# Audio tower on one core: small matmuls padded to 128, a hint at the loop's back branch, and new orders for the five engines

## The chip, the cores and the metric

The kernel runs on 1 core of one Trainium2 chip. The metric is device time in microseconds (us) for one execution, and the median of several executions is compared. Everything is float32.

## The reference, cut to what matters

32 clips of 625 frames with 128 samples each go through one DCT and four residual blocks:

```python
h = dct_frames(x)                                   # 625 -> 626 tokens of 128
h = h + bidirectional_mamba2(layernorm(h))          # conv with 4 taps, scan, gate, project
h = h + moe_top2_of_8_experts(layernorm(h))         # hidden 512, exact gelu
h = h + window_attention_8(layernorm(h))            # 8 heads of 16, 8 positions
h = h + pattern_ffn(layernorm(h))                   # gelu, top-64 of 512, gelu, top-128 of 256,
                                                    # softmax, values (256x64), 64 -> 512, top-64
```

In the last block `agg = softmax(top_p) @ process_values` has 64 columns and feeds `gelu(agg @ output_input_weights.T)`. In the Mamba block the depthwise convolution has 256 channels for x and 16 each for B and C, per direction. Every expert adds a bias b2 after its second matmul.

## The kernel before

Each clip is padded to 640 tokens, five tiles of 128. The work of a clip is cut into **four stages**: stage 1 is the DCT and the Mamba block, stage 2 the mixture of experts, stage 3 the window attention, stage 4 the pattern block. The stages are pipelined over clips: the trip of the loop for clip b runs stage 1 of clip b, stage 2 of clip b-1, stage 3 of clip b-2 and stage 4 of clip b-3. Three trips ahead of the loop and three behind it are written out; the loop `Fori(3, 32)` has 29 trips and so 28 taken back branches on each engine.

Every engine has a generator for each stage; a `yield` cuts it into **segments**. Below, "4.19" on an engine is segment 19 of its stage 4, counted from 0. `merged` takes segments in the order of a string of digits, one string for each engine, written out by hand or by a program outside the kernel: digit 4 means "the next segment of stage 4". An engine runs strictly in this order, and a segment that waits for a semaphore holds back all that stands behind it. So the strings alone set who waits for whom.

The segments that the text speaks of, with their lines:

- VectorE (DVE). Stage 1: 1.0 moments of h (L1031 to L1037); 1.1 to 1.4 the arithmetic of dt; from 1.5 on a scan of decays (L1072) and a weighing (L1080, L1083) for each of 12 chunks; 1.29 and 1.30 the Mamba output (L1094, L1102) and its moments. Stage 2: 2.0 moments; 2.1 to 2.3 gate, choice and slots; 2.4 adds the experts' answers (L1158, L1161), the last segment of a trip. Stage 3: 3.0 moments; 3.1 the logits (L1174 to L1180); 3.2 to 3.4 the softmax and values; 3.5 and 3.6 the residual (L1195, L1199) and moments. Stage 4: 4.1 to 4.8 the first top-64 of three tiles, in rounds of three MAX8 (L1219) and three MATCH_REPLACE8 (L1222), and 4.10 to 4.17 of two; 4.19 to 4.27 and 4.29 to 4.37 the split into pairs (L1241 on, L1249, L1252); 4.28 and 4.38 the weighing of it; 4.39 to 4.59 the last top-64; between them the outputs (L1281).
- TensorE (PE). 1.0 transposes x (L527), 1.1 the DCT, 1.5 to 1.43 twenty half units of convolution and gate (L566), 1.44 the wait for the last of them, then for each chunk B and C (L577), transposes (L584), the skip (L594) and the heads (L600); 1.93 to 1.95 project the output (L620, L628). 2.3 and 2.4 turn the routed rows (L663), then `up` (L675) and `down` (L684 with the bias, L686, L663) for 17 expert tiles. 4.1 to 4.5 the patterns (L747); 4.6 to 4.15 transposes (L754) and second matmuls (L762); 4.16 to 4.30 a chain of three for each tile (L772, L777, L782); then L791 and L796.
- ScalarE (ACT) evicts PSUM with the functions of each stage; Silu, Gelu and Exp live in different tables. Its segment 2.2 (L884, L888) reads 17 expert numbers into registers and starts three loads of weights.
- GpSimd (POOL) normalizes (`normalized`, L383 to L388), runs the attention's trees (L460 to L489), gates the Mamba output (L411), scatters and gathers the routed rows by indirect DMA (L442, L450). 1.5 and 1.6 scale the attention output of stage 1 (L425, L428), 1.7 adds it to h (L432, semaphore h1_done), 3.9 is stage 3's second normalization, 3.10 copies h3 into hk (L497).
- SyncE (SP) starts the remaining DMAs, among them the decays through DRAM and the routed rows (L339).

Of the kernel before, what the change touches and what calls it, by code (L numbers as in the profile page):

```python
# [13 lines left out]
P = 128  # L14
# [18 lines left out]
BC = 48  # L33
CW = 2 * P + BC
# [30 lines left out]
    ("ipT", NI), ("pwT", 4 * NP_), ("pv", 2 * HD), ("owT", NO), ("op", 4 * P),  # L65
# [7 lines left out]
for _name, _n in SETUP:  # L73
# [64 lines left out]
def audio_tower(nc, NB, consts_d, setup_d, x_d, out_d, rows_d, experts_d, routed_d, answers_d):  # L138
    ctx = ExitStack()
    with ctx:  # L140
# [64 lines left out]
        Bw = [sb(f"Bw{d}", [NS, CH, P]) for d in range(2)]  # L205
        Cs = [sb(f"Cs{d}", [NS, CH, WIN]) for d in range(2)]
# [46 lines left out]
        aggT = sb("aggT", [HD, P])  # L253
# [40 lines left out]
        def b2_of(i):  # L294
            return expert[i % WR][0:1, 8 * P + KB:EC]
# [58 lines left out]
        def run(engine, order, *stages):  # L354
# [4 lines left out]
            with engine.Fori(last, NB) as b:  # L359
# [140 lines left out]
        def _(pool):  # L500
# [10 lines left out]
            for d in range(2):  # L511
                nc.gpsimd.memset(Bw[d][:, :, WIN:P], 0.0)
# [9 lines left out]
        def pe_stage1(pe, b):  # L522
# [27 lines left out]
            for n in range(HALF_UNITS):  # L550
# [80 lines left out]
        def pe_stage2(pe, b):  # L631
# [47 lines left out]
            def down(i):  # L679
# [4 lines left out]
                nc.tensor.matmul(at, c("ones", 1), b2_of(i), start=True, stop=False)  # L684
# [53 lines left out]
        def pe_stage4(pe, b):  # L738
# [25 lines left out]
            for t in range(TILES):  # L764
# [11 lines left out]
                for j in range(2):  # L776
                    last = nc.tensor.matmul(pD[0:HD, 512:512 + P], c("pv")[:, j * HD:(j + 1) * HD], selT[:, j * P:(j + 1) * P],  # L777
# [4 lines left out]
                nc.tensor.matmul(pD[:, 0:NO], aggT[:], c("owT", HD), start=True, stop=True).then_inc(G["a3_ps"].s, 1)  # L782
# [659 lines left out]
```

## Time and profile before

| | us |
|---|---|
| median of 3 runs | 8329.64 |
| lowest and highest | 8313.04, 8416.84 |
| span of the profiled execution | 8631.7 |
| VectorE busy in it | 6951.3 |
| TensorE busy in it | 6340.7 |
| ScalarE, GpSimd busy in it | 3240.6, 3053.8 |

The profiled execution is one of its own, and its span is 302 us above the median of the runs; the prediction says where these lie. Its span runs from the first to the last instruction. The engines of the rows: PE is TensorE's matmul, PEld its loading of weights, DVE VectorE, ACT ScalarE, POOL GpSimd.

### The profile page before, as it was taken

Reading aid. Unit: us, or ns where it says so; the run is one execution under the profiler, and the core shown is the slowest. Engines: PE = TensorE matmul, PEld = TensorE weight load, DVE = VectorE, ACT = ScalarE, POOL = GpSimd, SP = SyncE. Lnnn points to the kernel's source line nnn. Section 1 sums busy time; section 2 is a strip of 40 time slices with the busy share of each in tenths; the row PEclk is TensorE's granted clock in tenths of the full one; section 3 lists DMA queues with packets and bytes.
Section 4 is the critical chain, followed back from the end, with each engine's and each line's share of the span. In section 5 each row is a group of like instructions: output and inputs, shape, how many; then the busy total and the mean of one; then the engine's idle time right before and its main releaser. Section 6 shows DMA issues by size and latency. Waiting matters only on the chain.

```text
span 8631.7 us, 109592 instructions
## 1 busy us (share of the span) xinstructions
PE 6340.7 (73%) x31240; PEld 4768.2 (55%) x31240; DVE 6951.3 (81%) x22124; ACT 3240.6 (38%) x7204; POOL 3053.8 (35%) x3190
## 2 busy tenths in 40 slices
PE   6777778777777777777777777777777777777633
PEld 4555556555565555555555555555555555555422
DVE  2377978878888878889887979788879787889787
ACT  2343334433444433444443334433334433344311
POOL 2343433333333334333333433333333333333320
PEclk8887777776787767788776778777778777788655
DMA  2321222211222212222221222212222211222200
GB/s 68 103 79 52 61 79 75 69 55 54 69 79 75 65 47 67 69 80 76 74 63 50 61 78 77 72 57 59 59 79 76 71 58 55 62 80 76 62 6 3
DMA packets 342763, 561.43 MB, mean 65 GB/s; under 512 B 33728, under 2 KB 261792, under 8 KB 341664
## 3 DMA queue, kind: packets, MB, share of 16 engines
q10 hardware_dynamic: 152576, 357.68, 13.4%
q1 hardware_dynamic: 168992, 153.36, 6.8%
q0 software_dynamic: 20480, 41.98, 1.6%
q8 instruction: 311, 5.10, 0.3%
q14 instruction: 404, 3.31, 0.1%
HBM read 484.15 MB, written 68.74 MB: 64 GB/s over the span
## 4 chain that ended last, share of the span: by engine, by line
DVE 52%; PE 20%; issue 14%; DMA 4%; POOL 4%; ACT 3%; another core or an unknown queue 1%; ACTq 1%; SPq 1%; DVEq 0%; POOLq 0%
DVE m L1219 10%; DVE work L1252 7%; DVE work L1222 6%; DVE sorted L1249 6%; DVE a L1222 3%; PE pS L566 3%; DMA rows<-routed_rows 3%; DVE lg L1174 2%; DVE ab L1072 2%; PE pM L675 2%; PE pS L628 2%; PE pD L762 2%; PE pM L686 1%; POOL u L388 1%; DVE Mt L1083 1%
## 5 line engine op out<-in xcount | busy, mean ns | idle before, releaser
L1219 DVE MAX8 m<-work 128x8 f32<-128x512 f32 x1792 | 1144.6, 680 | 1.0
L1222 DVE MATCH_REPLACE8 work<-m,work 128x512 f32<-128x512 f32 x1536 | 1025.9, 675 | 0.0
L566 PE MATMUL pS<-u_fm,wconv_s 128*128 128x315 f32 (+1 forms) x3072 | 966.6, 470 | 0.2
L675 PE MATMUL pM<-turned,expert 128*128 128x128 f32 x4352 | 739.8, 323 | 244.2 <-ACT turned L921 243.2
L675 PEld LDWEIGHTS pM<-turned,expert 128*128 128x128 f32 x4352 | 660.9, 229 | 346.2 <-issue 328.6
L686 PE MATMUL pM<-expert,hid 128*128 128x128 f32 x4352 | 798.3, 340 | 0.0
L908 ACT ACTIVATE hid<-pM,expert 128x128 f32<-128x128 f32 x2176 | 619.4, 367 | 385.6 <-PE pM L675 383.8
L460 POOL TENSOR_TENSOR lg<-lg,red 128x640 f32<-128x640 f32 x256 | 388.2, 1553 | 996.5 <-DVE red L1180 996.5
L566 PEld LDWEIGHTS pS<-u_fm,wconv_s 128*128 128x128 f32 (+1 forms) x3072 | 526.6, 179 | 387.2 <-issue 154.7
L686 PEld LDWEIGHTS pM<-expert,hid 128*128 128x128 f32 x4352 | 674.6, 237 | 81.9 <-issue 35.1
L1252 DVE MATCH_REPLACE8 work<-sorted,work 128x128 f32<-128x128 f32 x2240 | 591.5, 276 | 0.0
L1219 DVE MAX8 m<-a 128x8 f32<-128x512 f32 x768 | 504.4, 677 | 71.7 <-issue 70.2
L1249 DVE MAX8 sorted<-work 128x8 f32<-128x128 f32 x2560 | 541.7, 279 | 1.1
L411 POOL TENSOR_TENSOR yg<-xs,zs 128x525 f32<-128x525 f32 (+1 forms) x256 | 198.0, 806 | 962.7 <-ACT xs L863 951.6
L999 ACT COPY selT<-pD 128x512 f32<-128x512 f32 x160 | 93.6, 585 | 1169.8 <-PE pD L791 1008.2
L1072 DVE TENSOR_TENSOR_SCAN ab<-ab,cst 121x488 f32<-121x488 f32 x384 | 489.8, 1282 | 36.7 <-DMA ab<-decay_rows 36.7
L489 POOL TENSOR_TENSOR lg<-lg 128x640 f32<-128x640 f32 x224 | 362.6, 1642 | 440.3 <-DVE lg L1185 435.3
L466 POOL TENSOR_TENSOR red<-lg 128x640 f32<-128x640 f32 x128 | 197.8, 1582 | 748.0 <-ACT lg L951 748.0
L921 ACT COPY turned<-pM 128x256 f32<-128x256 f32 (+1 forms) x544 | 196.7, 362 | 699.6 <-issue 356.2
L1080 DVE TENSOR_TENSOR Xw<-pS,dts 121x256 f32<-121x256 f32 x384 | 157.9, 411 | 367.2 <-PE pS L584 362.6
L600 PE MATMUL pS<-Mt,Xw 121*64 121x121 f32 x3072 | 311.9, 336 | 163.0 <-DVE Mt L1083 163.0
L796 PE MATMUL pD<-cst,selT 128*128 128x128 f32 x1280 | 294.4, 401 | 185.7 <-ACT selT L999 130.8
(242 smaller groups left out, 14472.6 us busy)
## 6 DMA issues: line engine op xcount, KB each, us to landing
expert<-in_experts ACTq DMA_DIRECT2D x544, 578.0 KB
ab<-decay_rows SPq DMA_DIRECT2D x384, 230.7 KB
rows<-routed_rows SPq DMA_DIRECT2D x128, 256.0 KB, 4.8
answer_rows<-turned ACTq DMA_DIRECT2D x256, 128.0 KB, 3.9
x_sb<-in_x SPq DMA_DIRECT2D x32, 256.0 KB
out<-hk SPq DMA_DIRECT2D x32, 256.0 KB
routed_rows<-un,slot POOLq DMA_INDIRECT x320
rows<-answer_rows,slot POOLq DMA_INDIRECT x320
```

Source lines behind the costliest of these rows:

```text
L460: last = nc.gpsimd.tensor_tensor(lg[:, w, :], lg[:, w, :], red[:, 0, :], ALU.subtract)
L489: last = nc.gpsimd.tensor_tensor(lg[:, w, :], lg[:, w, :], lg[:, w + n, :], ALU.add)
L566: last = nc.tensor.matmul(pS[0:rows, 512 * (n % 3):512 * (n % 3) + HQ], wt, tap(d, i, half * HQ, HQ), start=(j == 0), stop=(j == len(block ...
L600: last = nc.tensor.matmul(pS[r * HD:(r + 1) * HD, B2 + g * WIN:B2 + (g + 1) * WIN], Xw[d][:, hh, :], Mt[d][:, hh, :], start=False, stop=(g ...
L675: last = nc.tensor.matmul(pM[:, bank(i) + j * P:bank(i) + (j + 1) * P], w1_of(i, j), turned[:, (i + 2) % 4, 1, :], start=True, stop=True)
L686: last = nc.tensor.matmul(at, hid[:, i % 2, j, :], w2_of(i, j), start=False, stop=(j == KB - 1))
L908: last = nc.scalar.activation(hid[:, i % 2, j, :], pM[:, at:at + P], ACT.Gelu, bias=b1_of(i, j))
L1072: nc.vector.tensor_tensor_scan(decays, decays, c("scan_src", WIN), 0.0, ALU.mult, ALU.add).then_inc(G["scanned"].s, 1)
L1219: link(nc.vector.max(m8[:, i, :], now[i]), len(tiles) - 1)
L1222: link(nc.vector.match_replace(work[i], m8[:, i, :], now[i], GONE), len(tiles) - 1)
L1249: link(nc.vector.max(top[:, 8 * r:8 * r + 8], left), 2 * n - 1)
L1252: link(nc.vector.match_replace(left, top[:, 8 * r:8 * r + 8], left, GONE), 2 * n - 1)
```

## The change

Six small operands are widened to 128. The convolution's unit for B and C gets 128 columns of weights in place of 48 (16 + 16 + 16), the rest zero (and the setup of wconv gets longer with it). B and C are kept on 128 partitions in place of 16, the rows below zeroed once by GpSimd at the start. The bias matmul of `down` contracts over 128 rows in place of 1 (rows of b2 below the first are zero). `pv` gets 128 columns in place of 64, so the aggregate comes on 128 partitions, and its product with `owT` contracts over 128 rows. The evictions by ScalarE stay, over 16 partitions for B and C, over 128 in place of 64 for the aggregate.

The loop is opened by `nc.Fori` for one engine with `hint_back_edge=True` in place of `engine.Fori`.

The five order strings are new. The segments themselves, their waits and their counts are unchanged.

```diff
-BC = 48
-CW = 2 * P + BC
+CW = 3 * P
-    ("ipT", NI), ("pwT", 4 * NP_), ("pv", 2 * HD), ("owT", NO), ("op", 4 * P),
+    ("ipT", NI), ("pwT", 4 * NP_), ("pv", 2 * P), ("owT", NO), ("op", 4 * P),
-PE_ORDER = ("14444143433323231111111111214141411134411111111111122424322112211114111111114111112242222122211221211221"
-            "114221111111112114211411112444241414112241111211144142114221412112244144143414434433")
-ACT_ORDER = ("44414334413233121111111113114141421111111111341111424223242112111111111111112424222224224422132221241212"
-             "14424214442144424122144244122421221114424144433")
-DVE_ORDER = ("34244414244211114442444444444434444444411111144444444441111111111433111411114444144444444434444441414343"
-             "42")
-POOL_ORDER = ("321421333333331121113314")
-SP_ORDER = ("1112221111111213443")
+PE_ORDER = ("44444411211113211114431211114144111111131131314143111141111112142221112341121111312122111122121222222211"
+            "122111212111122144114414144442412412211212111111124124111414214241211441441143434433")
+ACT_ORDER = ("44441111211141342144111111114213111311341143141111411411214111223111112211132322421221424222222223212124"
+             "14444444442421224422112214224414224111424114433")
+DVE_ORDER = ("34442144441411124424442444444444114444444113414141414144144444113114314111444114411411434444444444444431434"
+             "12")
+POOL_ORDER = ("321233333333111241331411")
+SP_ORDER = ("1112132211111121443")
@@
-        Bw = [sb(f"Bw{d}", [NS, CH, P]) for d in range(2)]
-        Cs = [sb(f"Cs{d}", [NS, CH, WIN]) for d in range(2)]
+        Bw = [sb(f"Bw{d}", [P, CH, P]) for d in range(2)]
+        Cs = [sb(f"Cs{d}", [P, CH, WIN]) for d in range(2)]
-        aggT = sb("aggT", [HD, P])
+        aggT = sb("aggT", [P, P])
-                lo, n = ((2 * P, BC), (0, P), (P, P))[unit]
+                lo, n = ((2 * P, P), (0, P), (P, P))[unit]
-            return expert[i % WR][0:1, 8 * P + KB:EC]
+            return expert[i % WR][:, 8 * P + KB:EC]
-            with engine.Fori(last, NB) as b:
+            with nc.Fori(last, NB, engines=[engine.engine], hint_back_edge=True) as b:
-                nc.gpsimd.memset(Bw[d][:, :, WIN:P], 0.0)
+                nc.gpsimd.memset(Bw[d][:], 0.0)
+                nc.gpsimd.memset(Cs[d][:], 0.0)
-                    last = nc.tensor.matmul(pS[0:rows, 512 * (n % 3):512 * (n % 3) + HQ], wt, tap(d, i, half * HQ, HQ),
+                    last = nc.tensor.matmul(pS[:, 512 * (n % 3):512 * (n % 3) + HQ], wt, tap(d, i, half * HQ, HQ),
-                nc.tensor.matmul(at, c("ones", 1), b2_of(i), start=True, stop=False)
+                nc.tensor.matmul(at, c("ones"), b2_of(i), start=True, stop=False)
-                    last = nc.tensor.matmul(pD[0:HD, 512:512 + P], c("pv")[:, j * HD:(j + 1) * HD], selT[:, j * P:(j + 1) * P],
+                    last = nc.tensor.matmul(pD[:, 512:512 + P], c("pv")[:, j * P:(j + 1) * P], selT[:, j * P:(j + 1) * P],
-                nc.tensor.matmul(pD[:, 0:NO], aggT[:], c("owT", HD), start=True, stop=True).then_inc(G["a3_ps"].s, 1)
+                nc.tensor.matmul(pD[:, 0:NO], aggT[:], c("owT"), start=True, stop=True).then_inc(G["a3_ps"].s, 1)
-                nc.scalar.copy(aggT[:], pD[0:HD, 512:512 + P]).then_inc(G["agg_sb"].s, 1)
+                nc.scalar.copy(aggT[:], pD[:, 512:512 + P]).then_inc(G["agg_sb"].s, 1)
```

What the new strings move, beside much that shifts by one or two places:

- VectorE, top of the trip: 3.0, 2.0, 4.1, 4.2, 4.3, 1.0, 4.4, 2.1, 4.5, 4.6, 2.2, 1.1 to 1.4, 4.7, 4.8, 2.3, 4.10 becomes 3.0, 4.1, 4.2, 2.0, 1.0, 4.3 to 4.6, 1.1, 4.7, 1.2 to 1.4, 2.1, 4.8, 2.2, 4.10 to 4.12, 2.3, 4.13.
- VectorE, middle: 3.1 goes from behind 4.19 to behind 1.9; the scans 1.5 and 1.6 from behind 4.27 to behind 4.21, the weighing 1.7 from behind them to behind 4.26, and 1.10 to 1.14 in among 4.28 to 4.33. End: "1.29, 4.59, 1.30, 3.5, 4.61, 3.6, 4.62, 2.4" becomes "4.59, 3.5, 1.29, 4.61, 3.6, 4.62, 1.30, 2.4".
- TensorE takes 4.1 to 4.5 ahead of 1.0; 4.11 ahead of 2.3; 2.14 to 2.21 in one run; 4.16 to 4.25 nearly in one run; 4.31 and 4.32 ahead of 1.90 to 1.92; 1.95 ahead of 3.8.
- ScalarE takes 4.4 behind 1.5 and 4.5 behind 3.0 (before: 4.4, 4.5, then 1.1), 2.1 behind them, and 4.35 ahead of 1.56 and 1.57.
- GpSimd takes the trees (3.1 to 3.8) ahead of 1.1, and 3.9, 3.10 ahead of 1.5 and 1.6.
- SyncE takes 1.3 ahead of 2.1.

## Rows read from the trace of the kernel before

**Rows 1.** The page: busy time of each engine.

```profile
PE 6340.7 (73%) x31240; PEld 4768.2 (55%) x31240; DVE 6951.3 (81%) x22124; ACT 3240.6 (38%) x7204; POOL 3053.8 (35%) x3190
```

**Rows 2.** Stretches (--windows): start:end, length, busy times, TensorE's clock, DMA.

```profile
0.00:776.00 776.00, 570.24 (x2998) 433.31 (x2998) 370.59 (x1105) 258.76 (x600) 264.82 (x306) 0.79 0.26 78
...
3384.70:3633.00 248.30, 187.07 (x976) 141.05 (x976) 216.19 (x692) 102.03 (x225) 95.55 (x99) 0.80 0.24 70
4382.80:4654.30 271.50, 214.76 (x976) 161.37 (x976) 218.02 (x692) 101.84 (x225) 96.85 (x99) 0.70 0.22 64
8019.50:8631.70 612.20, 267.87 (x914) 180.12 (x914) 509.53 (x1672) 129.53 (x304) 120.27 (x112) 0.58 0.08 24
```

**Rows 3.** Waits of VectorE in the trip 3384.7 to 3633.0: total, times, longest.

```profile
DVE work L1241 <- ACT a L971: 10.3, 1, 10.3
DVE h L1158 <- POOL hk L497: 6.2, 1, 6.2
DVE Xw L1080 <- PE pS L584: 3.4, 2, 2.3
DVE stats L1031 <- issue: 3.4, 2, 2.0
```

**Rows 4.** Waits of VectorE in the trip 4382.8 to 4654.3.

```profile
DVE Xw L1080 <- PE pS L584: 17.5, 5, 7.4
```

**Rows 5.** Timeline around a back branch: start, length, idle before and its releaser.

```profile
3384.24 0.27 ACT L957 COPY u4T<-pA 128x128 f32<-128x128 f32 x1 [0.56 <-PE pA L736]
3384.55 1.40 DVE L1161 SCALAR_TENSOR_TENSOR h<-rows,top,h 128x128 f32<-128x128 f32 x5
...
3387.82 1.32 PE L527 MATMUL pS<-cst,x_sb 128*128 128x128 f32 x5 [3.62 <-issue]
3387.95 0.87 DVE L1031 BATCH_NORM_STATS2 stats<-h 128x6 f32<-128x128 f32 x4 [2.00 <-issue]
...
3388.94 1.06 PE L747 MATMUL pD<-cst,u4T 128*128 128x512 f32 x1
...
3394.01 0.69 DVE L1219 MAX8 m<-a 128x8 f32<-128x512 f32 x1 [1.06 <-issue]
```

**Rows 6.** Timeline of the end of the next trip.

```profile
3620.18 1.17 POOL L383 TENSOR_TENSOR rstd<-vare,mhalf 128x5 f32<-128x5 f32 x1 [5.24 <-DVE vare L1037]
...
3630.08 1.25 POOL L497 TENSOR_TENSOR hk<-h,zero 128x640 f32<-128x640 f32 x1
...
3631.42 1.40 DVE L1158 SCALAR_TENSOR_TENSOR h<-rows,top,h 128x128 f32<-128x128 f32 x5 [6.23 <-POOL hk L497]
...
3632.86 0.35 DVE L1161 SCALAR_TENSOR_TENSOR h<-rows,top,h 128x128 f32<-128x128 f32 x1
```

**Rows 7.** Timeline ahead of VectorE's L1241.

```profile
3453.76 1.28 ACT L848 ACT_TABLE_LOAD   x1
...
3462.16 0.44 PE L663 MATMUL pM<-cst,rows 128*128 128x128 f32 x2 [3.21 <-DMA rows<-routed_rows]
...
3465.57 0.56 DVE L1241 TENSOR_TENSOR work<-a 128x384 f32<-128x384 f32 x1 [10.32 <-ACT a L971]
```

**Rows 8.** Timeline of ScalarE around segment 2.2.

```profile
3445.13 3.56 ACTq L888 DMA_DIRECT2D expert<-in_experts  x3
3448.04 0.52 ACT L853 ACTIVATE xs<-pS,cst 128x315 f32<-128x315 f32 x1 [9.57 <-issue]
```

**Rows 9.** Timeline of TensorE among expert tiles, at full clock.

```profile
3484.39 0.48 PE L577 MATMUL pS<-Cs,Bw 16*128 16x121 f32 x2
3484.80 0.44 PE L584 MATMUL pS<-cst,xs 128*128 128x128 f32 x2
...
3486.06 0.48 PE L684 MATMUL pM<-expert,cst 1*128 1x128 f32 x2
3486.47 1.16 PE L686 MATMUL pM<-expert,hid 128*128 128x128 f32 x8
3487.47 0.27 PE L663 MATMUL pM<-cst,rows 128*128 128x128 f32 x1
```

More of the change, by code:

```diff
@@ L94 @@
 )
-PE_ORDER = ("14444143433323231111111111214141411134411111111111122424322112211114111111114111112242222122211221211221"
-            "114221111111112114211411112444241414112241111211144142114221412112244144143414434433")
-ACT_ORDER = ("44414334413233121111111113114141421111111111341111424223242112111111111111112424222224224422132221241212"
-             "14424214442144424122144244122421221114424144433")
-DVE_ORDER = ("34244414244211114442444444444434444444411111144444444441111111111433111411114444144444444434444441414343"
-             "42")
-POOL_ORDER = ("321421333333331121113314")
-SP_ORDER = ("1112221111111213443")
+PE_ORDER = ("44444411211113211114431211114144111111131131314143111141111112142221112341121111312122111122121222222211"
+            "122111212111122144114414144442412412211212111111124124111414214241211441441143434433")
+ACT_ORDER = ("44441111211141342144111111114213111311341143141111411411214111223111112211132322421221424222222223212124"
+             "14444444442421224422112214224414224111424114433")
+DVE_ORDER = ("34442144441411124424442444444444114444414113141414144144444113114314111444114411411434444444444444431434"
+             "12")
+POOL_ORDER = ("321233333333111241331411")
+SP_ORDER = ("1112132211111121443")
 def merged(order, *stages):
@@ L563, in pe_stage1 @@
                 blocks = weights_of(d, unit)
-                rows = BC if unit == 0 else P
                 for j, (wt, i) in enumerate(blocks):
-                    last = nc.tensor.matmul(pS[0:rows, 512 * (n % 3):512 * (n % 3) + HQ], wt, tap(d, i, half * HQ, HQ),
+                    last = nc.tensor.matmul(pS[:, 512 * (n % 3):512 * (n % 3) + HQ], wt, tap(d, i, half * HQ, HQ),
                                             start=(j == 0), stop=(j == len(blocks) - 1))
@@ L847, in act_stage1 @@
                 if unit == 0:
-                    nc.scalar.activation(Bw[d][:, half * CH // 2:(half + 1) * CH // 2, NS:WIN], px[0:NS].rearrange("p (c t) -> p c t", c=CH // 2),
+                    nc.scalar.activation(Bw[d][0:NS, half * CH // 2:(half + 1) * CH // 2, NS:WIN], px[0:NS].rearrange("p (c t) -> p c t", c=CH // 2),
                                          ACT.Silu, bias=cb[0:NS, d, 2:3])
-                    last = nc.scalar.activation(Cs[d][:, half * CH // 2:(half + 1) * CH // 2, 0:Q], px[32:32 + NS].rearrange("p (c t) -> p c t", c=CH // 2),
+                    last = nc.scalar.activation(Cs[d][0:NS, half * CH // 2:(half + 1) * CH // 2, 0:Q], px[32:32 + NS].rearrange("p (c t) -> p c t", c=CH // 2),
                                                 ACT.Silu, bias=cb[32:32 + NS, d, 2:3])
@@ L1008, in _ @@
                 for ch in range(CH):
-                    nc.scalar.copy(Bw[d][:, ch, 0:NS], ident[0:NS, 0:NS])
-                    last = nc.scalar.copy(Cs[d][:, ch, Q:WIN], ident[0:NS, 0:NS])
+                    nc.scalar.copy(Bw[d][0:NS, ch, 0:NS], ident[0:NS, 0:NS])
+                    last = nc.scalar.copy(Cs[d][0:NS, ch, Q:WIN], ident[0:NS, 0:NS])
             last.then_inc(a_exp, 1)
@@ L1370, in bc @@
         gap = np.zeros(x.shape[:-1] + (NS,), x.dtype)
-        return np.concatenate([x[..., 0:272], gap, x[..., 272:288]], -1)
+        return np.concatenate([x[..., 0:272], gap, x[..., 272:288], np.zeros(x.shape[:-1] + (P - 3 * NS,), x.dtype)], -1)
     o["wconv"] = np.concatenate([bc(x[256:544].T) for x in w], 1)
@@ L1391, in laid_out @@
     o["pwT"] = a["L1_ffn_process_input_weights"].T.reshape(4, P, NP_).transpose(1, 0, 2)
-    o["pv"] = a["L1_ffn_process_values"].reshape(2, P, HD).transpose(1, 0, 2)
+    pv = a["L1_ffn_process_values"].reshape(2, P, HD).transpose(1, 0, 2)
+    o["pv"] = np.concatenate([pv, np.zeros_like(pv)], -1)
     o["owT"] = a["L1_ffn_output_input_weights"].T
```

## The prediction

> **What bounds the kernel now.** First the page's busy times [rows 1]: VectorE leads with 81%, TensorE follows with 73%, so neither is full. Then stretches of the trace [rows 2], to see whether the profiled execution is a typical one. The body of the loop ends on VectorE with the adds of L1161, so the time from one such group to the next is a trip: 3384.55 to 3632.86, 248.3 us [rows 5, 6]. Another trip took 271.5 us [rows 2]. VectorE's work is the same in both (216 and 218 us busy), TensorE's clock is not: 0.80 against 0.70, and with it TensorE is busy 215 us in place of 187. The waits tell where that hurts: VectorE waited 17.5 us at L1080 for TensorE's transposes in the long trip, 3.4 us in the short one [rows 3, 4].
>
> The loop covers 776.0 to 8019.5, 28 trips of 258.7 us on average. With every trip short the execution would take 776.0 + 28 x 248.3 + 612.2 = 8340.6 us, 0.1% from the median of 8329.64. So the runs shown consist of short trips, and the 291 us by which the profiled span exceeds 8340.6 are long ones. I sum against the short trip and 8340.6, and take 11 us off at the end for the median.
>
> In the short trip VectorE is the engine to watch: 216.2 us busy, 32 us idle. Its waits [rows 3]: 10.3 us at L1241 for ScalarE's gelu of the third tile, 6.2 us at L1158 for GpSimd's copy hk, 3.4 us at L1080 for TensorE, 3.4 us at L1031 for nothing that the trace shows; the rest are small ones. 248.3 - 32 = 216 us is the floor of a trip that no order can pass.
>
> **Step 1, the back branch.** VectorE's adds end at 3385.95; the next instruction starts after 2.00 us of "issue", and with a second gap inside the same group this makes the 3.4 us [rows 3, 5]. TensorE shows 3.62 us of "issue" at the same place. The Trainium skill, "Runtime: NRT & Kernel Launch", section on instruction fetch, says that a taken branch whose target is not in the window has to fetch the page first; the trace agrees as far as these gaps sit only there. The hint should start that fetch early. From the adds' end to the first MAX8 it is now 8.1 us: 3.4 + 1.1 us of gaps and 3.6 us for two groups of moments. After the change TensorE takes the patterns (4.1 to 4.5) first. u4T is there at 3384.51 [rows 5], three tiles of patterns take 4.2 us at a rising clock, 5.1 at a low one (6 matmuls of 0.85), their gelu 0.6: the first MAX8 can start at 3390.2, 4.3 us behind the adds, and only one group of moments (1.8) is done by then. Net -(8.1 - 4.3 - 1.8) = **-2.0 us**. Bounds: 0 if the hint does nothing here, -3.4 if every gap goes and the clock is high. A second gap that stays is hidden under the wait for the patterns.
>
> **Step 2, the end of the trip.** GpSimd starts its two long segments at 3620.18, and hk is done at 3631.33 [rows 6]; 1.5 and 1.6 take the first 6.3 us of it, 3.9 and 3.10 the last 4.8. The new string puts 3.9 and 3.10 first, and VectorE takes 3.6 ahead of 1.30, so hk is ready 4.9 us behind 3.6, while VectorE still has 4.62 and 1.30, 4.9 us. The wait of 6.2 us goes. What is late next: 3.5 now stands ahead of 1.29, and TensorE's 3.8 behind 1.95, so VectorE waits there for the projection's norm (L628) as it did at 1.29, and 4.61 behind it waits for its output. I count 1.2 us for that: **-5.0 us**, bounds -6.2 and -2. 1.7 on GpSimd, and so h1_done, comes 8 us behind 1.30; its waiters, 1.0 on ScalarE and 2.0 on VectorE, now stand behind the patterns and two rounds of MAX8 and aren't reached earlier. The gathers (2.2) keep their place.
>
> **Step 3, the gate and the third tile.** TensorE's 4.11 waited behind 2.3, which waited 3.21 us for the routed rows [rows 7]; it now stands ahead. Against that stands ScalarE's path. 4.4 and 4.5 are gelus, 1.7 is a silu, 2.1 an exponent, and every change of function costs a table load of 1.28 us [rows 7]. Behind 1.5 ScalarE now takes load, 4.4, load, 1.7, 3.0, load, 4.5, load, 2.1: 4 x 1.28 + 0.6 + 1.05 + 0.6 + 0.6 + 0.2 = 8.2 us, while VectorE has 2.1 and 4.8, 4.7 us, before 2.2 asks for the exponent: a new wait of 3.5 us. 2.3, which gives the tile numbers, moves behind three more rounds (2.5 us each), and ScalarE's 2.2 cannot read its 17 numbers earlier: from the eviction before it to the one behind it are 9.57 us, 3.56 of them issues of weights [rows 8]. TensorE's convolution stands still for that, as now. Adding this up, a2 of the third tile comes 77.7 us behind the adds (79.6 now), and VectorE is there 6.6 us early. 3.5 + 6.6 = 10.1 against 10.3: **0 us**, bounds -6 (the rows of step 1 and no wait at 2.2) and +3.
>
> **Step 4, the middle.** VectorE reaches its first weighing, 1.7, now 23 us behind the start of 4.19 (2.0 + 7 rounds of 2.7 + 2 scans of 1.1), in place of 38. It needs all 20 evictions of the convolution. From L1241's start to the second chunk's transposes it took 19.7 us [rows 7, 9]; the new ScalarE string has 7 changes of table in that stretch in place of 3, and two half units of convolution of 2.3 us more lie in it on TensorE: some 27 us, a wait of 4 us. 4.28 waits for ScalarE's 4.17, which stands behind 1.47 and so behind the second chunk: 3 us. 4.39 waits for three gelus a3, whose chain of L772, L777 and L782 starts only behind the second cut (4.18 on ScalarE), and that cut is later by the four scans and weighings put ahead of it: 7 us. Gone are the 3.4 us at L1080 and 0.7 at L1174. The sum, 10 us, charges each hand-over in full and one behind the other; the lower end is 0, when TensorE keeps ahead. The nearest rows are the waits of this kind in the short trip, 3.4 us [rows 3]. I take **+5 us**.
>
> **Step 5, the padding.** At full clock a bias pair with one row costs 3486.47 - 3486.06 = 0.41 us, and the pair of `down` behind it again starts slowly: the ten matmuls from L684 to L663 take 1.41 us [rows 9]. Eight of them are plain, at 0.11 us each from one to the next, so a uniform run would take about 1.1: 0.3 us for each of 17 tiles. L577 with 16 rows costs 0.41 us where 0.22 would do, and slows the transposes behind it: 0.35 us for each of 12 chunks. pv, owT and the convolution's unit 0 give 2 us together. That is 11 to 12 us less of TensorE in a trip, most of it where VectorE doesn't wait. It counts in the chains of steps 3 and 4 and ahead of L620: **-4 us**, bounds 0 and -8. The Trainium skill, "TensorE: Matmul & The Clock Gate", part 3 on packing small matmuls, says that a matmul with K = 32 takes the same time as one with K = 128, so that padding would gain nothing; the rows show the same length for one matmul (0.27 to 0.28 us) but a longer distance where the shape changes. By the rule the step is 0 and the sum comes to 8260.
>
> **Step 6, outside the loop.** The written-out trips have no branch; their orders change too. GpSimd zeroes 2 x 1494 columns more at the start, some 2.7 us at the rate of its other memsets, ahead of SyncE's first writes. I take -10 us in all, bounds -30 and +10.
>
> **The sum.** -2.0 - 5.0 + 0 + 5 - 4 = -6 us in a trip, 242.3 us; 28 x -6 = -168; 8340.6 - 168 - 10 - 11 = 8152, rounded to 8150 us, 2.2% below the median. For the profiled execution itself, with as many long trips as now, 8631.7 - 178 = 8454; I don't expect the trips to be long as often, since TensorE has less to do.
>
> **Rivals.**
> (a) The middle holds: steps 3 and 4 at their lower ends, -6 and 0 us. For it: VectorE's segments of different stages are spread more evenly. Against it: the table loads of step 3. The trip is 248.3 - 2 - 5 - 6 - 4 = 231 us, the time 7830; with half of it 7950.
> (b) The other side: ScalarE's table loads. By its new string ScalarE changes tables 25 times in a trip, 19 before; 6 x 1.28 = 7.7 us in the same stretches in which TensorE waits for its evictions and VectorE for TensorE. It decides once the waits of step 4 are above 11 us: then the gain of steps 1, 2 and 5 is used up. At its full price (10 + 7.7 us of waits in the middle, padding off the path) the trip is 248.3 - 7 + 17.7 = 259, the time 8620; half of that excess gives 8480. For it: the waits at L1241 and L1080 are of this make. Against it: ScalarE is busy only 102 of 248 us [rows 2].
> (c) The hint does nothing. Then TensorE starts the patterns 3.6 us later and the gain of step 1 is gone: 8150 + 28 x 2 to 28 x 3.6, 8210 to 8250.
> (d) Padding gains nothing: 8260.
>
> **Chances.** The forecast's own range is 8000 to 8300, chance 0.48; (a) 0.20, (b) 0.15, (c) 0.07, (d) 0.10. A measurement of this kernel tells about 2% from no change, 8163 and 8496. Of the forecast half lies below 8163, with (a) this gives 0.46 faster; 0.45 within 2%; of (b) somewhat over half lies above 8496, 0.09 slower. For 8 times in 10 the range goes from 7870 to 8440.
>
> **What the changed profile would show.** Step 1: no "issue" at L1031 behind the adds, at most 1.5 us; L747 as TensorE's first work. Step 2: no wait of L1158 for hk. Step 3: a wait at L1121 (2.2) of 3 to 4 us for ScalarE, 5 to 8 us at L1241's line. Step 4: waits at L1080 and at the first memset of 4.39, 5 to 14 us together. Step 5: the distance from the bias pair to L663 1.1 to 1.2 us. The prediction is wrong if waits in the middle of the trip sum to far less than 10 or more than 20 us, or if TensorE's clock settles at another mean than 0.8: by [rows 2] a trip at 0.70 costs 23 us more.

## The result, and the profile after

The changed kernel took 8712.74 us (8704.41 to 8725.52) where the kernel before took 8339.6 in the same session. The ratio, taken over the fast runs of both, is 1.0412, 95% interval 1.0348 to 1.0477 (the two medians alone would give 1.045). It is slower; the prediction said 8150 us and at most 8440.

The page first. This is its line of busy times, to be held against [rows 1]:

```profile
PE 5898.8 (68%) x31240; PEld 4686.8 (54%) x31240; DVE 7646.1 (88%) x22124; ACT 3451.0 (40%) x7380; POOL 3191.5 (37%) x3192
```

TensorE's busy time fell by 442 us, as padding was to do; its mean granted clock is 0.78 here and was 0.75 before, which shortens it too. VectorE runs the same 22124 instructions as before and is busy 695 us longer. No step of the prediction has a term for that. A trip in the middle of the loop (the table by windows: length, then busy time and instructions of each engine, granted clock, DMA share, GB/s) against the two trips of [rows 2]:

```profile
3375.60:3638.40 262.80, 184.95 (x977) 148.30 (x976) 239.40 (x692) 109.09 (x231) 99.63 (x100) 0.78 0.22 66
```

The trip is 262.8 us, VectorE busy 239.4 of them in place of 216.2, and idle 23.4 in place of 32. So the waits did shrink. Here are those of that trip for other engines, against [rows 3]:

```profile
DVE work L1240 <- ACT a L970: 5.2, 1, 5.2
DVE sm L1120 <- ACT lgt L877: 3.9, 1, 3.9
DVE h L1194 <- PE pA L722: 3.3, 1, 3.3
DVE Xw L1079 <- PE pS L583: 2.6, 1, 2.6
DVE hk L1280 <- PE pD L795: 2.5, 3, 1.1
DVE a L1265 <- ACT a L983: 1.5, 1, 1.5
```

Which instructions grew? The costliest groups with shapes kept apart have each mean duration; all of the run, after:

```profile
L1265 DVE TENSOR_TENSOR_SCAN a<-minus,a 128x256 f32<-128x256 f32 x160 | 285.7, 1832 | 59.1 <-ACT a L983 59.1
L1184 DVE TENSOR_TENSOR lg<-lg,v 128x640 f32<-128x640 f32 x128 | 225.7, 1821 | 2.9 <-POOL red L465 2.9
L1269 DVE SCALAR_TENSOR_TENSOR a<-a,sums 128x256 f32<-128x256 f32 x160 | 224.6, 1450 | 2.3
L1272 DVE SCALAR_TENSOR_TENSOR a<-a 128x256 f32<-128x256 f32 x160 | 134.8, 886 | 3.2
L1267 DVE TENSOR_SCALAR sums<-sums 128x3 f32<-128x3 f32 x32 | 45.6, 1425 | 1.1
L1248 DVE MAX8 sorted<-work 128x8 f32<-128x128 f32 x2560 | 539.8, 277 | 1.2
```

The same lines in the kernel before, each one number higher:

```profile
L1266 DVE TENSOR_TENSOR_SCAN a<-minus,a 128x256 f32<-128x256 f32 x160 | 98.7, 668 | 28.8 <-ACT a L984 28.8
L1185 DVE TENSOR_TENSOR lg<-lg,v 128x640 f32<-128x640 f32 x128 | 97.0, 820 | 0.0
L1270 DVE SCALAR_TENSOR_TENSOR a<-a,sums 128x256 f32<-128x256 f32 x160 | 69.0, 481 | 2.3
L1273 DVE SCALAR_TENSOR_TENSOR a<-a 128x256 f32<-128x256 f32 x160 | 60.5, 423 | 3.2
L1268 DVE TENSOR_SCALAR sums<-sums 128x3 f32<-128x3 f32 x32 | 5.4, 169 | 1.1
L1249 DVE MAX8 sorted<-work 128x8 f32<-128x128 f32 x2560 | 541.7, 279 | 1.1
```

Five lines grew by 187 + 129 + 156 + 74 + 40 = 586 us, most of the 695; a TENSOR_SCALAR on three columns went from 0.17 to 1.43 us. MAX8, nearly a third of VectorE's work with all its lines, didn't change (279 and 277 ns). What ran beside those that grew? The timeline of VectorE's segment 4.28 (start, duration, engine, line), with GpSimd's row that covers it; equal instructions in a row are one line:

```profile
3497.63 11.84 POOL L459 TENSOR_TENSOR lg<-lg,red 128x640 f32<-128x640 f32 x7
3497.81 5.66 DVE L1265 TENSOR_TENSOR_SCAN a<-minus,a 128x256 f32<-128x256 f32 x3 [1.47 <-ACT a L983]
3503.39 1.43 DVE L1266 TENSOR_TENSOR sums<-sums 128x3 f32<-128x3 f32 x1
3504.86 1.47 DVE L1267 TENSOR_SCALAR sums<-sums 128x3 f32<-128x3 f32 x1
3506.36 3.78 DVE L1269 SCALAR_TENSOR_TENSOR a<-a,sums 128x256 f32<-128x256 f32 x3
...
3510.20 0.42 DVE L1272 SCALAR_TENSOR_TENSOR a<-a 128x256 f32<-128x256 f32 x1
```

GpSimd's subtraction of the maximum ends at 3509.47, and from there on VectorE's instructions take 0.42 us again. In the kernel before that subtraction had been over for 15 us when 4.28 began:

```profile
3480.39 12.04 POOL L460 TENSOR_TENSOR lg<-lg,red 128x640 f32<-128x640 f32 x8 [30.56 <-DVE red L1180]
...
3507.34 1.83 DVE L1266 TENSOR_TENSOR_SCAN a<-minus,a 128x256 f32<-128x256 f32 x3
```

In the new order only 1.10, one scan, stands between 4.28 and 3.1, which releases the subtraction. The same holds 38 us later: 3.2 (L1184) runs beside L479, and 4.38 beside the value tree, L488. That gave the first theory, a collision; the rival was that these instructions are slow where they now stand for some other reason.

### The profile page after: what moved, and what is told of

Its sections match the earlier page's. It is cut to its first block, busy times and chain, and to the rows that moved or that the text cites. A ratio compares the mean times of both kernels' runs of the same rounds, so it can differ in the third digit from the quotient of the medians.

```text
span 8723.7 us, 109912 instructions
## 1 busy us (share of the span) xinstructions
PE 5898.8 (68%) x31240; PEld 4686.8 (54%) x31240; DVE 7646.1 (88%) x22124; ACT 3451.0 (40%) x7380; POOL 3191.5 (37%) x3192
## 4 chain that ended last, share of the span: by engine, by line
DVE 53%; PE 23%; ACT 12%; issue 7%; ACTq 3%; POOL 1%; DMA 1%; DVEq 0%; SPq 0%; POOLq 0%
DVE m L1218 11%; PE pS L565 7%; DVE work L1221 7%; DVE a L1221 4%; DVE ab L1071 4%; DVE a L1265 3%; DVE work L1251 3%; DVE sorted L1248 3%; DVE a L1269 3%; DVE lg L1184 3%; PE pD L761 2%; PE pD L795 2%; DVE Mt L1082 2%; ACT L907 2%; DVE a L1272 2%
## 5 line engine op out<-in xcount | busy, mean ns | idle before, releaser
L674 PE MATMUL pM<-turned,expert 128*128 128x128 f32 x4352 | 789.7, 339 | 451.7 <-ACT turned L920 397.9
L674 PEld LDWEIGHTS pM<-turned,expert 128*128 128x128 f32 x4352 | 704.8, 244 | 596.4 <-issue 543.5
L459 POOL TENSOR_TENSOR lg<-lg,red 128x640 f32<-128x640 f32 x256 | 450.4, 1793 | 1550.0 <-DVE red L1179 1550.0
L565 PE MATMUL pS<-u_fm,wconv_s 128*128 128x315 f32 x3072 | 984.2, 475 | 0.0
L565 PEld LDWEIGHTS pS<-u_fm,wconv_s 128*128 128x128 f32 x3072 | 641.6, 213 | 254.7 <-issue 73.5
L685 PE MATMUL pM<-expert,hid 128*128 128x128 f32 x4352 | 707.0, 316 | 0.0
L599 PEld LDWEIGHTS pS<-Mt,Xw 121*64 121x64 f32 x3072 | 184.5, 157 | 567.6 <-DVE Mt L1082 526.4
L761 PE MATMUL pD<-cst,selT 128*128 128x256 f32 x1280 | 372.7, 441 | 98.4 <-ACT selT L967 98.3
L488 POOL TENSOR_TENSOR lg<-lg 128x640 f32<-128x640 f32 x224 | 397.9, 1799 | 41.4 <-DVE lg L1184 35.9
L761 PEld LDWEIGHTS pD<-cst,selT 128*128 128x128 f32 x1280 | 275.0, 220 | 179.3 <-ACT selT L967 125.4
```

The lines of the kernel that those rows point to most:

```text
L459: last = nc.gpsimd.tensor_tensor(lg[:, w, :], lg[:, w, :], red[:, 0, :], ALU.subtract)
L565: last = nc.tensor.matmul(pS[:, 512 * (n % 3):512 * (n % 3) + HQ], wt, tap(d, i, half * HQ, HQ), start=(j == 0), stop=(j == len(blocks) - 1))
L599: last = nc.tensor.matmul(pS[r * HD:(r + 1) * HD, B2 + g * WIN:B2 + (g + 1) * WIN], Xw[d][:, hh, :], Mt[d][:, hh, :], start=False, stop=(g ...
L674: last = nc.tensor.matmul(pM[:, bank(i) + j * P:bank(i) + (j + 1) * P], w1_of(i, j), turned[:, (i + 2) % 4, 1, :], start=True, stop=True)
L685: last = nc.tensor.matmul(at, hid[:, i % 2, j, :], w2_of(i, j), start=False, stop=(j == KB - 1))
L761: last = nc.tensor.matmul(pD[:, 512:512 + NP_], selT[:, j * P:(j + 1) * P], pw[:, j, :], start=(j == 0), stop=(j == 3))
```

## The experiments

orders_only, pad_hint_old and tail_new ran on a chip on which the kernel before took 8709 us, not 8340 to 8372 as on the others, and TensorE was granted less (0.79 of full clock in the loop of pad_hint_old, 0.82 for the same kernel on another chip). So ratios to the kernel before on the same chip are compared throughout. The last columns come from the windows of the loop's 28 trips in each profiled run.

| run | median us | ratio to before, 95% | mean trip | VectorE busy in it | idle |
|---|---|---|---|---|---|
| before | 8340 | 1 | 258.7 | 216.8 | 41.9 |
| after | 8713 | 1.0412 (1.0348 to 1.0477) | 262.7 | 239.2 | 23.5 |
| hint_only | 8183 | 0.9761 (0.9721 to 0.9801) | 244.4 | 216.3 | 28.1 |
| pad_only | 8137 | 0.9718 (0.9693 to 0.9743) | 243.1 | 217.0 | 26.1 |
| trees_no_read | 8277 | 0.9890 (0.9863 to 0.9917) | 247.6 | 221.4 | 26.2 |
| before_pool_reads | 8579 | 1.0258 (1.0198 to 1.0318) | 255.4 | 220.4 | 35.0 |
| orders_only | 9299 | 1.0723 (1.0631 to 1.0814) | 283.0 | 237.8 | 45.1 |
| pad_hint_old | 8410 | 0.9707 (0.9624 to 0.9790) | 252.2 | 217.1 | 35.1 |
| tail_new | 8399 | 0.9682 (0.9600 to 0.9765) | 252.2 | 218.1 | 34.1 |
| trees_gone | 8132 | 0.9739 (0.9688 to 0.9791) | 243.0 | 216.1 | 26.9 |
| weigh_first | 8422 | 1.0061 (1.0023 to 1.0099) | 252.2 | 229.5 | 22.7 |
| weigh_apart | 8559 | 1.0250 (1.0196 to 1.0304) | 256.6 | 224.3 | 32.3 |
| pad_hint_again | 8027 | 0.9611 (0.9560 to 0.9661) | 239.0 | 217.1 | 21.9 |

For before and after the profiled span is 8631.7 and 8723.7 us. The profiled run of before is 292 us longer than its median run, that of after 11 us, so the gap in mean trips understates the loss.

**1. hint_only.** The kernel before with one line changed:

```
-            with engine.Fori(last, NB) as b:
+            with nc.Fori(last, NB, engines=[engine.engine], hint_back_edge=True) as b:
```

> The kernel before with the hint on the loop's back branch alone. The prediction's step 1 gives -2.0 us a trip (0 to -3.4), so about 8275 us, 8230 to 8340. If the idle time behind the branch is hidden by other waits of the same trip, 8330 to 8345.

Measured: 183 us less, 6.5 us a trip; 8183 us lies below the expected 8230. The gap at L1031 is gone, and the 3.62 us of "issue" ahead of TensorE's L527 [rows 5] are 0.33. VectorE's own gaps were only 3.4 us [rows 3]. The rest is at its waits for TensorE and ScalarE, whose branches were hinted too.

**2. pad_only.** The changed kernel with the old order strings and the old loop line.

> The kernel before with the padding of the small matmuls alone, old orders and no hint. The prediction's step 5 gives -4 us a trip (0 to -8): about 8210 us, 8080 to 8340. If VectorE's own work sets the trips between its waits, the shorter distances of TensorE show only where VectorE waits for it and the time is 8300 to 8345.

Measured: 228 us less. Not all of it is the loop's: in the profiled runs the loop starts at 729 us in place of 776, and what follows it takes 604 us in place of 612. That is 55 us, and leaves 6.2 us a trip, between the 4 of the step and its upper bound of 8. The trips are all 242 to 245 us; no long ones are left. The granted clock is 0.80 over the whole run, where the kernel before has 0.757 to 0.764 on that chip. How much of the gain is the shorter distance between matmuls and how much the clock, no run separates.

**3. trees_no_read.** GpSimd as busy as in after, but writing only:

```
-            for w in range(AW):
-                last = nc.gpsimd.tensor_tensor(lg[:, w, :], lg[:, w, :], red[:, 0, :], ALU.subtract)
-            last.then_inc(G["lg_done"].s, 1)
+            fill(pool, b, 0, lg[:, 0:AW, :]).then_inc(G["lg_done"].s, 1)
```

with `fill` three memsets in a row, each behind a one-column addition, and the same at L479 and L488.

> The changed kernel with GpSimd's subtraction of the maximum, its half of the weighting and the three sums of the value tree (lines 459, 479 and 488) replaced by memsets of the same tile that keep GpSimd about as long at work but read nothing; the attention's output is therefore zero, all else is computed. Theory one, a collision: VectorE's instructions with two operands from SBUF take up to three times as long while GpSimd's instructions that read SBUF run, and all of the 23 us that VectorE's work grew in a trip are this. Then VectorE's work falls from 239.4 to 217 to 220 us a trip, lines 1269 and 1272 go back to 480 and 420 ns, and the time to 8040 to 8150 us. The Trainium skill (SBUF, Who interferes with whom) has such instructions contend against GpSimd's reads alone; if its writes counted as much, the time would stay at 8600 us or more. Theory two: these instructions run long where the new order puts them whatever GpSimd does (ScalarE's writes of the same tiles just before them, say): 8680 to 8740 us and 239 us a trip.

Measured: VectorE's work 221.4 us a trip, not 217 to 220, and 8277 us, more than expected though far from 8600. Two things explain it. The first shows in the timeline of 4.28:

```profile
3338.47 4.36 POOL L396 MEMSET lg<- 128x5120 f32 x1
3341.01 1.85 DVE L1270 TENSOR_TENSOR_SCAN a<-minus,a 128x256 f32<-128x256 f32 x3 [2.46 <-ACT a L988]
3342.78 0.14 DVE L1271 TENSOR_TENSOR sums<-sums 128x3 f32<-128x3 f32 x1
...
3342.95 4.48 DVE L1272 TENSOR_SCALAR sums<-sums 128x3 f32<-128x3 f32 x1
3343.04 4.37 POOL L396 MEMSET lg<- 128x5120 f32 x1
3347.46 1.28 DVE L1274 SCALAR_TENSOR_TENSOR a<-a,sums 128x256 f32<-128x256 f32 x3
```

The three scans run beside a memset at full speed (1.85 us for what was 5.66), and the addition of two operands starts as that memset ends (0.14 us for what was 1.43). The TENSOR_SCALAR of three columns, one operand, stands still for a whole memset and ends with it. The second is 3.2:

```profile
L1189 DVE TENSOR_TENSOR lg<-lg,v 128x640 f32<-128x640 f32 x128 | 195.2, 1582 | 2.9 <-POOL red L474 2.9
```

It takes 1.58 us in place of the 0.82 of before, four times a trip. GpSimd's sums of the denominator (L474 to L483), which read SBUF, are still in this kernel, and 3.2 meets them. That is 3 us a trip, and the TENSOR_SCALARs of 4.28 and 4.38 are 2: together about the 4.6 us by which 221.4 exceeds the 216.8 of before. So the form matters on both sides, and theory two is out: place and tiles are those of after. Against after, VectorE's work fell by 17.8 us a trip and its trip by 15.

**4. before_pool_reads.** In the old order, 12 of these behind GpSimd's subtraction:

```
+                nc.gpsimd.tensor_tensor(spare_out[:], spare_in[:], spare_in[:], ALU.add).then_inc(G["spare"].s, 1)
```

> The kernel before with 12 further additions of 128x640 from a spare tile to a spare tile on GpSimd, right behind its subtraction of the maximum (line 460), where it had been idle for 24 us; nothing else waits for them. Theory one, the collision: the first weigh_pairs segment of VectorE (lines 1266 to 1273), which starts 15 us behind that subtraction, grows from 4.9 to 11 to 14 us and the time to 8490 to 8620 us. Theory two: VectorE's durations stay and the time is 8320 to 8360 us.

Measured: 2.6% slower, inside the range, but not where I expected it. The additions took 1.25 us each when alone, so the twelve were over 1.1 us into 4.28; that segment grew by 1 us only. The scans ahead of it met them instead, 1.43 us in the mean where the kernel before has 1.28:

```profile
L1079 DVE TENSOR_TENSOR_SCAN ab<-ab,cst 121x488 f32<-121x488 f32 x336 | 479.3, 1433 | 0.0
```

In all VectorE's work grew by 3.6 us a trip, and the time by more. The collision can be made in the old order too; its price there is not settled by this run, since its waits moved as well and its granted clock was lower (0.739 to 0.749, before 0.757 to 0.764).

**5. ports.** The disputed cost by itself: VectorE's form times GpSimd's form, four instructions against four, started together.

> A kernel of its own that computes nothing of the reference (its output is zero). Eight forms of VectorE instruction, four of each in a row, start together with four GpSimd instructions of 640 columns: none, an addition of two SBUF tiles, a tensor_scalar of one, a memset. Theory one: scan and scalar_tensor_tensor with two operands from SBUF, and the addition of three columns, each wait for one whole GpSimd instruction when that reads SBUF (mean 1.2 to 1.9 us instead of 0.1 to 0.5), and not beside the memset; max and reduce with one operand never do. The 4.5 us of line 1272 in the kernel with memsets say that tensor_scalar of five columns does wait beside a memset. With one operand in PSUM the scalar_tensor_tensor is not slowed. The Trainium skill (SBUF, Who interferes with whom) states the same division. Theory two: the slowing comes from this kernel's tiles or order, and here every form has the mean that it has beside an idle GpSimd.

The costliest groups (the tile's name gives VectorE's form, then what GpSimd was doing: `idle`, `read_two` an addition of two tiles of 640 columns, `read_one` a TENSOR_SCALAR of one, `write` a memset):

```profile
L100 DVE SCALAR_TENSOR_TENSOR stt_two_sbuf_read_two<-a,b 128x256 f32<-128x256 f32 x4 | 5.4, 1418 | 0.3 <-POOL gb L240 0.3
...
L116 DVE TENSOR_SCALAR ts_five_read_two<-a 128x5 f32<-128x5 f32 x4 | 3.1, 840 | 1.8 <-POOL gb L268 1.8
L120 DVE TENSOR_TENSOR tt_three_read_two<-a,b 128x3 f32<-128x3 f32 x4 | 3.1, 830 | 3.3 <-POOL gb L275 3.3
L132 DVE SCALAR_TENSOR_TENSOR stt_two_sbuf_read_one<-a,b 128x256 f32<-128x256 f32 x4 | 3.0, 806 | 5.0 <-POOL gb L296 5.0
...
L68 DVE SCALAR_TENSOR_TENSOR stt_two_sbuf_idle<-a,b 128x256 f32<-128x256 f32 x4 | 1.4, 417 | 0.4 <-POOL gb L200 0.4
L164 DVE SCALAR_TENSOR_TENSOR stt_two_sbuf_write<-a,b 128x256 f32<-128x256 f32 x4 | 1.4, 420 | 1.8 <-POOL gb L352 1.8
...
L104 DVE SCALAR_TENSOR_TENSOR stt_psum_sbuf_read_two<-pq,b 128x256 f32<-128x256 f32 x4 | 1.4, 418 | 1.8 <-POOL gb L247 1.8
...
L124 DVE MAX8 max_one_read_two<-a 128x8 f32<-128x256 f32 x4 | 1.4, 416 | 3.3 <-POOL gb L282 3.3
...
L180 DVE TENSOR_SCALAR ts_five_write<-a 128x5 f32<-128x5 f32 x4 | 0.7, 582 | 0.3 <-POOL gb L380 0.3
L84 DVE TENSOR_SCALAR ts_five_idle<-a 128x5 f32<-128x5 f32 x4 | 0.4, 167 | 0.3 <-POOL gb L220 0.3
...
L184 DVE TENSOR_TENSOR tt_three_write<-a,b 128x3 f32<-128x3 f32 x4 | 0.4, 157 | 2.1 <-POOL gb L387 2.1
```

Two operands from SBUF beside a reading GpSimd: 0.42 becomes 1.42 us; the scan, not shown, goes from 0.67 to 1.64. Beside a memset: unchanged. One operand in PSUM, or a MAX8: unchanged beside anything. A TENSOR_SCALAR with its operand in SBUF waits beside reads and writes, 0.17 to 0.84 and 0.58. The cost goes by the length of GpSimd's instruction: beside the shorter `read_one` (0.73 us alone) the 256 columns lose 0.39 us, beside the addition (1.53 us alone) 1.00. It hardly goes by VectorE's size: of the four additions of three columns, two last 1.50 us, a whole addition of GpSimd's, and two 0.15, as they do alone. Their mean of 0.83 is below the 1.2 that I expected. GpSimd loses too: its addition takes 1.53 us alone and up to 1.93 against scans. Theory one holds on tiles that have nothing to do with this kernel.

The Trainium skill, "SBUF — State Buffer", section "Who interferes with whom", says that an instruction of VectorE with two SBUF inputs contends with a GpSimd instruction that reads SBUF and not with one that only writes, and, of VectorE's modes that use both ports, that whoever comes first holds the shared pair for its whole instruction. The runs agree with the first in each form tried here; to the second the runs add that the wait for a whole instruction is seen with two operands as well. It would have named this loss ahead of the change.

**6 and 7. orders_only and pad_hint_old,** together with tail_new on one chip: the diff's two halves. The first is the kernel before with the five new strings; the second the changed kernel with the five old ones.

> The kernel before with the new orders alone, no padding and no hint. Hint and padding gave 183 and 228 us where they stood alone. If the three parts add up, the orders alone take 8713 + 183 + 228, about 9120 us. If VectorE's own work, which the collisions with GpSimd make 239 us a trip whatever TensorE does, bounds the trips, hint and padding are worth less under these orders, and it takes 8760 to 8950 us. Either way VectorE works 239 us a trip and lines 1266, 1270 and 1273 run beside line 460 and 489 of GpSimd.

> The changed kernel with the old orders: padding and hint together. If the two gains add up, 8366 - 183 - 228, about 7955 us, and trips of 238 to 241 us. If both take the same idle time, because the hint's gain was in trips that a slower TensorE held up, 8050 to 8140 us.

Measured: 1.0723 and 0.9707. Their product is 1.041, the ratio of the whole change. So the new orders cost 7.2%, padding and hint give 2.9% back, and they act one on top of the other. The orders cost VectorE 21 us of work a trip (237.8 against 216.8). As ratios to 8366 us my two expectations for orders_only were 1.09 and 1.05 to 1.07; with an interval to 1.081 the parts may overlap a little, but they are all there. For pad_hint_old I expected 0.951 if the two gains add up and 0.962 to 0.973 if they share some idle time; 0.9707 says the latter. The granted clock of orders_only is lower than that of before on this chip (0.72 against 0.74 to 0.755), so its 7.2% holds some of that too.

**8. tail_new.** pad_hint_old with the part of the new end that step 2 rests on: 1.30 last on VectorE, 3.9 and 3.10 first on GpSimd. 1.29 and TensorE's string stay as before:

```
-DVE_ORDER  ... 1 4 1 4 3 4 3 4 2      POOL_ORDER ... 1 1 2 1 1 1 3 3 1 4
+DVE_ORDER  ... 1 4 4 3 4 3 4 1 2      POOL_ORDER ... 1 1 2 1 3 3 1 1 1 4
```

> Padding, hint and old orders, but for the end of the trip: VectorE does 1.30 behind 3.5, 3.6 and 4.62, and GpSimd 3.9 and 3.10 ahead of 1.5 and 1.6. The prediction's step 2 gives -5.0 us a trip (-2 to -6.2) against padding and hint alone, so 130 to 150 us less than that kernel, 60 at least. The rival: the wait for hk at line 1157 goes, but the first stage's chain through lines 419 to 431 comes 6 us later and VectorE waits for it at the trip's start; then the gain is under 50 us.

Measured: 11 us less of 8410, within the intervals of each other. The rival is right. VectorE's waits in pad_hint_old, over the whole run (in total, times, longest):

```profile
DVE h L1157 <- POOL hk L496: 193.0, 31, 8.0
...
DVE hk L1280 <- PE pD L795: 162.8, 60, 4.3
```

and in tail_new:

```profile
DVE hk L1280 <- PE pD L795: 261.9, 92, 4.3
...
DVE stats L1030 <- POOL h L431: 99.3, 32, 8.1
```

The wait for hk, 193 us, is gone. Of it 99 came back at L1280, and another 88 at the first norm of the next trip, whose operand of L431 now comes later (11.0 us in pad_hint_old).

**9. trees_gone.** The changed kernel with GpSimd's part of the attention reduced to one instruction of one column in each segment, and the exponential of zero.

> The changed kernel with GpSimd's whole part of the attention (lines 459 to 488: subtraction of the maximum, sums of the denominator, its half of the weighting, value tree) left out but for one instruction of one column in each segment, and the exponential taken of zero; the attention's output is not the reference's. If the collisions are the whole loss and the prediction's other terms hold, VectorE works 216 to 218 us a trip, waits 22 to 25, and the time is 8712 - 31 x 22, about 8000 to 8080 us where the kernel before takes 8340 (0.96 to 0.97 of it). If something else in the new orders costs time that the collisions hide, for one the further ACT_TABLE_LOADs, the waits grow and the time stays above 8300 us (0.995).

Measured: VectorE 216.1 us a trip, its floor; 0.9739, which is 8122 us for the 8340 of the first comparison. The collisions are the whole 23 us of work, and of the 23.7 us by which a trip of after exceeds one of pad_hint_again they make 19.7 (262.7 less 243.0). The waits are 26.9 us and the ratio is 0.004 above the range, a little more than expected.

**10 and 11. weigh_first and weigh_apart.** In VectorE's string of after, `... 1.16 3.2 1.17 1.18 4.38 3.3 ...` becomes

```
... 1.16 1.17 1.18 4.38 3.2 3.3 ...
```

and weigh_apart also has `1.9 1.10 4.28 4.29 3.1 1.11` for `1.9 3.1 1.10 4.28 1.11 4.29`, with ScalarE's 4.16 and 4.17 ahead of its 2.12.

> The changed kernel, but VectorE takes 3.2 and 3.3 behind 4.38 instead of 3.2 ahead of 1.17. 3.2 releases GpSimd's value tree (line 488), so 4.38 (lines 1265 to 1272) runs before that tree and beside only the end of line 479. Theory one: 3.2 goes from 6.6 to 3 us, 4.38 from 12.2 to 6 to 8, about 8 us less a trip, 8420 to 8520 us where after takes 8712 and before 8340, a ratio of 1.010 to 1.022. Theory two, that the place in the order doesn't matter: 1.035 to 1.045.

> weigh_first, and besides VectorE takes 1.10, 4.28 and 4.29 ahead of 3.1, which releases GpSimd's subtraction (line 459), and ScalarE does 4.16 and 4.17 ahead of 2.12, so that 4.28's operands are there 8 us earlier. 4.28 goes from 13.8 to 5 us for a wait ahead of it of up to 5 us where 1.5 stands now: 4 to 9 us less a trip than weigh_first, a ratio of 0.98 to 1.005 to the kernel before. If what the collisions took comes back as waits (GpSimd's trees are now later, beside 3.2 and 4.37), no less than weigh_first.

weigh_first: one segment, 3.2, went behind three others, and 1.0412 became 1.0061, 3.4% or 10.5 us a trip, somewhat more than I expected. The timeline shows 4.38's second half and 3.2 at full speed, since GpSimd's tree only starts behind 3.2:

```profile
3417.08 3.42 DVE L1264 TENSOR_TENSOR_SCAN a<-minus,a 128x256 f32<-128x256 f32 x2
3420.43 0.13 DVE L1265 TENSOR_TENSOR sums<-sums 128x2 f32<-128x2 f32 x1
...
3420.79 0.88 DVE L1268 SCALAR_TENSOR_TENSOR a<-a,sums 128x256 f32<-128x256 f32 x2
...
3422.76 3.03 DVE L1183 TENSOR_TENSOR lg<-lg,v 128x640 f32<-128x640 f32 x4
```

weigh_apart missed: 1.025, outside the expected 0.98 to 1.005 and slower than weigh_first. 4.28 did fall to 4.9 us, and VectorE's work by 5.2 us a trip. But its idle time rose by 9.6. Its waits:

```profile
DVE a L1263 <- ACT a L981: 297.1, 63, 11.5
DVE Xw L1077 <- PE pS L581: 273.5, 83, 17.7
```

In weigh_first these are 72.2 and 181.2 us. VectorE waits 6.6 us for 4.28's operands, not up to 5, and the attention, 8 to 15 us later on GpSimd, meets 4.38 again (8.9 us in the mean in place of 6.6). The expectation's last sentence is what happened.

**12. pad_hint_again.** The kernel of run 7 on the chip of runs 9 to 11.

> Padding and hint with the old orders once more, on the chip of the other three: 0.965 to 0.975 of the kernel before. It tells which order is the better one at equal padding and hint: trees_gone at or above this ratio would mean that the new orders bring nothing even without the collisions, 0.02 or more below it that they would have been the gain.

Measured: 0.9611, a little below the expected 0.965, and the fastest kernel of the study, with trips of 239.0 us. The same kernel has 0.9707 on the other chip; had the gains of runs 1 and 2 added up, it would be 0.949. trees_gone stands at 0.9739 beside it: at equal padding and hint, the new orders are 1.3% slower than the old ones even without the collisions, and that although trees_gone is also spared GpSimd's tree work and the waits for it.

## Why the prediction was wrong

**The step that failed** is the frame: "VectorE's work is the same in both", said of two trips of one order, became "216 us is the floor of a trip", and every step then moved waits over a fixed 216. As a floor it held: no run went below it. As a constant it didn't. All terms are terms of waiting, and growth of VectorE's work was put at nothing without a reason. The order moved something else, which GpSimd instruction runs beside which VectorE instruction, and that changed the work by 23 us a trip, four times the gain that I summed. No rival had it: (b) put the loss on ScalarE's table loads.

It was there to be seen. The trace of before shows the weigh and 3.2 segments all in gaps of GpSimd's, and where a scan of L1072 runs beside GpSimd's arithmetic it takes 1.53 us in the mean and up to 2.5 (125 of 384), and never over 1.18 elsewhere; a spread within one group, with shapes kept apart, was the sign. "Ask what runs beside it" was done for waits, never for durations.

**The baseline.** 8340.6 us for 28 short trips lies next to the median, but that does not show what the prediction read from it, that the runs consist of short trips. By [rows 2] such a run would have a mean clock of 0.78; the runs of this kernel on record between 8312 and 8395 us have 0.757 to 0.767. What their trips look like is not on record. It moves the start of the sum, not the terms in a trip.

**Step 1** was mis-sized, -2.0 against -6.5 us a trip alone. I added up what VectorE saves at the branch. TensorE's and ScalarE's branches are hinted too, and their 3.6 us come out at VectorE's later waits: for L1241 hint_only shows 228.7 us, before 316.9 (some of it in the long trips of that run).

**Step 2** held in its first half only. The wait for hk is gone, as said. What is late next I put at 1.2 us; after shows 3.3 at L1194 and 1.8 more at L1280 behind it, and tail_new shows that the part of the step on VectorE and GpSimd gives 11 us in all, where the step had 140.

**Step 3** came out: 3.9 us at L1120 (3.5 said), 5.2 at L1240 (6.6).

**Step 4** also, for the first two waits: 2.6 us at L1079 (4), 1.5 at L1265 (3). The 7 us at 4.39 did not come; with the collisions VectorE got there late, and in trees_gone, without them, it waits 0.8 us. The chain that I charged there was not that long.

**Step 5**: the distance came as said. At full clock the matmuls from the bias pair to the next tile's first now take 3511.18 - 3510.07 = 1.11 us, against 1.41 in [rows 9]:

```profile
3510.07 0.39 PE L683 MATMUL pM<-expert,cst 128*128 128x128 f32 x2
...
3511.18 0.27 PE L662 MATMUL pM<-cst,rows 128*128 128x128 f32 x1
```

Its worth was 6.2 us a trip in place of 4, with a clock of 0.80 in place of 0.76 in it, and 55 us outside the loop, where the step had nothing. Rival (d) is out: padding alone is 2.8% faster. What the step cites from the Trainium skill, "TensorE: Matmul & The Clock Gate", on one matmul with K = 32 stands in its section "Why this matters for your kernels", not in part 3.

**Step 6** said -10 us outside the loop, bounds -30 and +10. In after the loop starts at 750.5 us in place of 776.0, and what follows it takes 617.3 in place of 612.2: -20 us, inside the bounds. Padding alone gave more than all three parts together.

**Small slips.** Half of rival (a) would be 7990 us, not 7950, and half of the forecast with (a) is 0.44, not 0.46. The traces have 24 table loads a trip after and 18 before, not 25 and 19; the six more were right.

**The sum** without the collision would have looked right: 8150 said, 8122 from trees_gone's ratio. That is luck. Padding and hint together gave 345 us in pad_hint_again, twice what steps 1 and 5 held (168), and the orders took 105 of it back where steps 2 to 4 came to nothing.

**Rival (b)**, the only one on the slow side, is not shown as a cause: the further table loads are in trees_gone too, which is 2.6% faster than before. They are inside its 3.7 us a trip against pad_hint_again, with the wait at L1120 the plainest part; what share is theirs was not tried apart.

## What to carry to other kernels

An order written out by hand decides not only who waits for whom but what runs beside what, and between VectorE and GpSimd that changes durations: before segments are moved, list VectorE's instructions that take two operands from SBUF (and its TENSOR_SCALARs), list GpSimd's, and keep them apart; one segment moved behind three others was worth 3.4% here. But look at the waits too: weigh_apart took collisions away and lost more in waiting. When an engine's busy time grows at an equal count of instructions, compare the mean duration group by group before any wait. A change that bundles safe gains with a new order should be measured in its two halves: 0.961 was lying inside 1.041.

## What the runs showed of the hardware

- The loss goes by GpSimd's instruction more than by VectorE's: an addition of three columns costs 1.43 us beside a subtraction of 640 columns (after), 0.16 beside memsets (ports).
- A TENSOR_SCALAR of three columns, one operand, stood still for 4.48 us beside one memset of 5120 columns, while scans with two operands ran past it.
- GpSimd pays as well: the subtraction at L459 went from 1.55 to 1.79 us in the mean.
- The hint on the back branch was worth 2.4% of the kernel's time with 28 taken branches, more than the gaps that VectorE's rows show there.
- Zeroes that widen six small matmul operands to 128 made the kernel 2.8% faster, with a granted clock of 0.80 in place of 0.76, while TensorE was not the busiest engine.
